# Graph layer with experts: output rows updated by an accumulating scatter in place of gather, add and scatter

## The chip, the cores and the metric

The kernel runs on one core of a Trainium2 chip. The metric is the time of one execution in microseconds of the device; the number for a kernel is the median of its runs. Five engines run side by side and are ordered only by semaphores: TensorE (PE, matmuls; PEld is its weight load), VectorE (DVE), ScalarE (ACT), GpSimd (POOL) and SyncE (SP), which issues most of the DMAs. The DMAs with indices are issued by GpSimd. All transfers share 16 DMA engines.

## What is computed

For 1250 nodes of 1024 features: a layer norm, then x + graph attention (20000 edges) + linear attention, then x + a mixture of 8 experts on the layer norm of that sum. Only the last part is touched by the change:

```python
x = x + gnn(xn, ...) + mix(xn, ...)
# experts, on the layer norm of x
scores = jnp.maximum((x @ gate_W + gate_b) / TEMP, EPS)
p = jax.nn.softmax(scores, axis=-1)
_, topk_idx = jax.lax.top_k(p, K)                      # K = 2 of E = 8
topk_mask = jax.nn.one_hot(topk_idx, E).sum(-2) > 0
w = jnp.maximum(p, W_THRES)
w = w / jnp.take_along_axis(w, topk_idx, axis=-1).sum(-1, keepdims=True)
comb = jnp.where(topk_mask, w, 0)
y = jnp.einsum('bsd,edf->bsef', x, expert_W) + expert_b
out = jnp.einsum('bsef,bse->bsf', y, comb) / K
x = x + out
```

All matmuls of weights are done with each float32 operand split in two parts, `hi` and `lo`, and three products.

## The kernel before

The kernel runs one stage after the other: the Gram matrix and linear attention, the attention table of the edges, the graph attention, then the layer norm and the gate, and last the experts. Up to the experts, `out` in HBM has been filled with x + graph attention + linear attention (line 529), and the normed rows lie in `xn2_d`.

**Routing (lines 1280 to 1361, VectorE).** Each of the 2500 pairs (token, chosen expert) gets a slot. Slots are ordered by expert, and every expert has whole blocks of 128 slots, at least one. `g_pos` is the slot of a pair. Slots that no pair fills are empty places; they stand at the end of an expert's last block. Two sets of small matmuls (line 1647, line 1666) turn positions into tables by slot: `tok_of` (which token), `slot_f` (the same as a float, -1 for an empty place), `row_of` (the output row; an empty place gets a row over N) and `w_slot` (its weight). `bounds` holds the first block of each expert. For these inputs the trace shows 23 blocks: experts 0 and 1 have one block each, expert 2 has eight (blocks 2 to 9), expert 3 one (block 10), experts 4 and 5 five each (11 to 15 and 16 to 20), experts 6 and 7 one each. This is read from where the casts of expert weights stand between the blocks.

**Experts.** Each engine has a loop over experts and, inside it, one over that expert's blocks.

- SP loads the weights of an expert as eight pieces of 512 KB into `e_raw[k]` (`load_expert`, line 531). There is one set of eight buffers: piece k of the next expert can be issued when VectorE has made `e_lo[k]` of the present one (`s_elo`). `load_bias` issues the bias.
- ScalarE casts them to `e_hi` (line 843, `expert_hi`), two buffers: expert e+1 is cast when all blocks of expert e-1 are multiplied. For each block it casts the transposed tokens to `lt_hi` (line 848) in two halves.
- VectorE, at the start of expert e and before its first block, makes `e_lo` of expert e+1 (line 1369, `expert_lo`, eight instructions). In block i it then does: the first half of `lt_lo` of block i+1 (line 1374), the two halves of `yb` = matmul result + bias (line 1421), the second half of `lt_lo`, and `y` = `yb` times `w_slot` plus `res` (line 1428). This order is fixed; a wait at `y` holds back everything after it.
- TensorE, in block i: 24 matmuls of the first half of the contraction, the 8 transposes of block i+1 (line 1655), 24 matmuls of the second half. It waits for `lt_lo` of its block (`s_llo`), and before it overwrites the result it waits for `yb` of the block before (`s_ye`).
- GpSimd, in block i: gathers the tokens of block i+2 into `gx` (line 654), gathers the output rows of block i into `res` (line 673), waits for `y` and scatters it to `out` (line 681), and skips rows over N. Blocks of one expert name different rows, so a gather of `res` needs to wait only for the scatter of the last block of the expert before (`s_sc` at `first_block[e]`, line 668). `y`, `res`, `gx` and `yb` each have one buffer.

Of the kernel before, what the change touches and what calls it, by code (L numbers as in the profile page):

```python
# [12 lines left out]
def gps_layer(nc, x, src, dst, gnn_W, gnn_a, w_ql, w_qr, w_key, w_value, gate_W, gate_b, expert_W, expert_b, out):  # L13
# [44 lines left out]
    with ctx:  # L58
        def at(name, word, shape, dt=f32):
            return nc.alloc_sbuf_tensor_at(name, shape, dt, offset=base + 4 * word)  # L60
# [133 lines left out]
        res = at("res", SMALL - D, [P, D])  # L194
# [71 lines left out]
        al_bc = at("al_bc", SH, [P, 2, P])  # L266
        al2 = small("al2", [P, NH, NT])
# [9 lines left out]
        row_now = small("row_now", [P, 1], i32)  # L277
# [115 lines left out]
        s_row, s_put, s_res, s_sum2, s_sc = sem("s_row"), sem("s_put"), sem("s_res"), sem("s_sum2"), sem("s_sc")  # L393
# [171 lines left out]
        def _(pool):  # L565
# [79 lines left out]
            for i in range(2):  # L645
                pool.wait_ge(s_xn2d[i], 16 * (NT // 2))
                pool.wait_ge(s_x2s[i], 16 * (NT // 2))
            pool.wait_ge(s_route, 1)
# [9 lines left out]
            first_block = [pool.value_load(bounds[0:1, e:e + 1], min_val=0, max_val=NBLK) for e in range(NE + 1)]  # L658
            pool.wait_ge(s_tr, 2)
            gather(1)  # L660
            pool.wait_ge(s_wslot, 1)
            pool.dma_start(res[:, :], out[0:P, :]).then_inc(s_sc, 16)
            for e in range(NE):

                with pool.Fori(first_block[e], first_block[e + 1]) as i:
                    pool.wait_ge(s_tr, i * 2 + 4)
                    gather(i + 2)
                    pool.wait_ge(s_sc, first_block[e] * 16 + 16)
                    pool.sem_inc(s_passed, 1)
                    nc.gpsimd.tensor_copy(row_now[:, :], row_of[:, bass.ds(i, 1)]).then_inc(s_row, 1)  # L670
                    pool.wait_ge(s_row, i + 1)
                    pool.sem_inc(s_passed, 1)
                    nc.gpsimd.indirect_dma_start(out=res[:, :], out_offset=None, in_=out,
                                                 in_offset=bass.IndirectOffsetOnAxis(ap=row_now[:, :], axis=0),
                                                 bounds_check=N - 1, oob_is_err=False).then_inc(s_res, 16)
                    pool.wait_ge(s_sum2, i + 2)
                    pool.sem_inc(s_passed, 1)
                    nc.gpsimd.tensor_copy(row_put[:, :], row_of[:, bass.ds(i, 1)]).then_inc(s_put, 1)
                    pool.wait_ge(s_put, i + 1)
                    pool.sem_inc(s_passed, 1)  # L680
                    nc.gpsimd.indirect_dma_start(out=out, out_offset=bass.IndirectOffsetOnAxis(ap=row_put[:, :], axis=0),
                                                 in_=y[:, :], in_offset=None,
                                                 bounds_check=N - 1, oob_is_err=False).then_inc(s_sc, 16)
            pool.wait_ge(s_gx, first_block[NE] * 16 + 32)
# [4 lines left out]
        def _(act):  # L689
# [167 lines left out]
            nc.scalar.activation(g_p[:, :, :], g_p[:, :, :], ACT.Exp).then_inc(s_gexp, 1)  # L857
            act.wait_ge(s_route, 1)
# [16 lines left out]
        def _(dve):  # L875
# [457 lines left out]
            link(V.tensor_tensor(g_place[:, :], g_cum[:, :], g_nb[:, :], ALU.subtract))  # L1333
            link(V.scalar_tensor_tensor(g_place[:, :], g_place[:, :], float(P), ps[:, 7, 0:NE], ALU.mult, ALU.add))
            link(V.scalar_tensor_tensor(g_place[:, :], g_place[:, :], -1.0, g_ends[:, 0:NE], ALU.add, ALU.subtract))
            link(V.tensor_tensor(g_pos[:, :, :], g_run[:, :, :].rearrange("p e t -> p t e"), over_tiles(g_place[:, :]), ALU.add))
# [68 lines left out]
            for g in range(2):  # L1405
                block_lo(0, g)
# [304 lines left out]
```

## Time and profile before

| | us |
|---|---|
| runs of the kernel before | 1359.47, 1359.84, 1362.1 (median 1359.84) |
| the profiled execution, its own time | 1355.7 |
| its span (first to last instruction) | 1353.4 |
| TensorE busy, share of the span | 1208.8 (89%) |
| VectorE | 757.0 (56%) |
| GpSimd | 441.8 (33%) |
| ScalarE | 306.0 (23%) |
| mean granted TensorE clock, share of full speed | 0.947 |

The experts' matmuls begin at 1021 us and end at 1342 us of the span. Times of start are counted from the start of the span. In the rows below a line gives the engine, the line of the kernel, the operation, what it writes and reads, and how many instructions were merged (`x8`). In brackets stands how long the engine was idle before and what ended the idle time. PE durations are those of one matmul from in to out and overlap; starts of matmuls in a row are what counts.

### The profile page before, as it was taken

The numbers are of one execution on the slowest core, as the hardware profiler recorded it, in microseconds if no ns is written. First come the engines' busy times: TensorE is split into PE (matmuls) and PEld (weight loads), VectorE is DVE, ScalarE is ACT, GpSimd is POOL, SyncE is SP. The second block draws the span as 40 slices with busy tenths as digits, with TensorE's granted clock in tenths as the row PEclk, the third lists the DMA queues.
The fourth block names the chain that finished last, engine by engine and source line by source line (L and its number), as shares of the span: only waits on it lengthen the run. The fifth ranks groups of instructions, "written<-read, shape, count | busy, mean of one in ns | idle before, by whom it ended". The sixth has DMA issues, their size and how long they took to land.

```text
span 1353.4 us, 16130 instructions
## 1 busy us (share of the span) xinstructions
PE 1208.8 (89%) x5789; PEld 1015.2 (75%) x5789; DVE 757.0 (56%) x1496; ACT 306.0 (23%) x410; POOL 441.8 (33%) x432
## 2 busy tenths in 40 slices
PE   5979799998999999999979999799937699889894
PEld 4878577776878899988967878688726588768683
DVE  7777531346333777767643247777567633553434
ACT  2321111113111111111012323233335211503030
POOL 4800587878784000000000035444202233233222
PEclk9989899998999999999989999799958799989997
DMA  5010241652412222211134441333358844663641
GB/s 190 17 47 1 87 128 37 219 159 73 125 15 80 82 82 83 96 51 57 51 103 141 136 125 70 121 106 119 125 207 314 331 139 134 231 233 128 236 138 60
DMA packets 89703, 165.02 MB, mean 122 GB/s; under 512 B 15468, under 2 KB 45926, under 8 KB 89508
## 3 DMA queue, kind: packets, MB, share of 16 engines
q1 hardware_dynamic: 74148, 129.76, 28.0%
q0 software_dynamic: 15488, 34.39, 8.6%
q8 instruction: 39, 0.64, 0.2%
q14 instruction: 28, 0.23, 0.0%
HBM read 125.53 MB, written 42.04 MB: 124 GB/s over the span
## 4 chain that ended last, share of the span: by engine, by line
PE 55%; DVE 13%; DMA 13%; issue 11%; POOL 5%; ACT 1%; POOLq 1%; DVEq 0%; SPq 0%; ACTq 0%
PE ps L1444 17%; PE ps L1445 17%; PE ps L1446 17%; DMA res<-out,row_now 9%; DMA out<-y,row_put 2%; DVE y L1428 2%; PE ps L1567 2%; POOL x_in L633 1%; DVE e_lo L1369 1%; DVE run L959 1%; PE ps L1629 1%; DVE w_lo L887 1%; DVE xt_lo L895 1%; DVE place_sum L1007 1%; DVE place L1005 1%
## 5 line engine op out<-in xcount | busy, mean ns | idle before, releaser
L595 POOL DMA_INDIRECT tab_d<-val_i,addr_i x160 | 213.5, 1334 | 144.7 <-issue 144.7
L1444 PE MATMUL ps<-e_hi,lt_hi 128*128 128x512 f32 x368 | 151.9, 413 | 41.6 <-DVE lt_lo L1374 41.6
L1446 PE MATMUL ps<-e_hi,lt_lo 128*128 128x512 f32 x368 | 147.9, 402 | 0.0
L1445 PE MATMUL ps<-e_lo,lt_hi 128*128 128x512 f32 x368 | 147.8, 402 | 0.0
L1444 PE MATMUL ps<-xt_hi,q_hi 128*128 128x416 f32 (+1 forms) x384 | 142.4, 371 | 0.0
L1445 PE MATMUL ps<-xt_lo,q_hi 128*128 128x416 f32 (+1 forms) x384 | 135.3, 352 | 0.0
L613 POOL TENSOR_TENSOR att_part<-att 128x640 f32<-128x640 f32 x10 | 16.9, 1687 | 362.1 <-PE ps L1446 358.1
L1446 PE MATMUL ps<-xt_hi,q_lo 128*128 128x416 f32 (+1 forms) x384 | 134.9, 351 | 0.0
L1444 PEld LDWEIGHTS ps<-e_hi,lt_hi 128*128 128x128 f32 x368 | 72.4, 197 | 58.8 <-DVE lt_lo L1374 44.5
L1134 DVE TENSOR_TENSOR cnt<-ps,cnt 128x256 f32 x208 | 87.7, 422 | 42.3 <-PE ps L1567 27.7
L1114 DVE TENSOR_SCALAR hot_s<-iota_g,s_tab 128x256 f16<-128x256 f16 x208 | 63.4, 305 | 39.9 <-PE ps L1567 39.1
L1428 DVE SCALAR_TENSOR_TENSOR y<-yb,w_slot,res 128x1024 f32<-128x1024 f32 x23 | 29.5, 1285 | 99.0 <-DMA res<-out,row_now 99.0
L1446 PEld LDWEIGHTS ps<-e_hi,lt_lo 128*128 128x128 f32 x368 | 71.8, 195 | 16.0
L1445 PEld LDWEIGHTS ps<-e_lo,lt_hi 128*128 128x128 f32 x368 | 72.6, 197 | 14.5
L848 ACT CAST lt_hi<-ps 128x512 fp32r<-128x512 f32 x48 | 28.1, 585 | 240.8 <-PE ps L1655 129.4
L1444 PE MATMUL ps<-h_hi,att_hi 128*128 128x512 f32 (+1 forms) x200 | 80.4, 402 | 0.0
L1445 PE MATMUL ps<-h_lo,att_hi 128*128 128x512 f32 (+1 forms) x200 | 79.5, 397 | 0.0
L1446 PE MATMUL ps<-h_hi,att_lo 128*128 128x512 f32 (+1 forms) x200 | 79.2, 396 | 0.0
L1369 DVE TENSOR_TENSOR e_lo<-e_raw,e_hi 128x1024 fp32r<-128x1024 f32 x64 | 73.4, 1221 | 4.1 <-ACT e_hi L843 4.1
L1444 PEld LDWEIGHTS ps<-xt_hi,q_hi 128*128 128x128 f32 x384 | 72.4, 188 | 1.8
L1445 PEld LDWEIGHTS ps<-xt_lo,q_hi 128*128 128x128 f32 x384 | 72.6, 189 | 0.5
L1446 PEld LDWEIGHTS ps<-xt_hi,q_lo 128*128 128x128 f32 x384 | 72.1, 188 | 0.5
(281 smaller groups left out, 2629.3 us busy)
## 6 DMA issues: line engine op xcount, KB each, us to landing
e_raw<-in_L_ffn_expert_W SPq DMA_DIRECT2D x64, 512.0 KB, 7.5
acc<-in_x SPq DMA_DIRECT2D x18, 512.0 KB, 7.8
w_raw<-in_L_mix_w_key SPq DMA_DIRECT2D x16, 512.0 KB
h_d<-hs SPq DMA_DIRECT2D x18, 256.0 KB
q_in<-q_d SPq DMA_DIRECT2D x9, 512.0 KB, 4.9
h_in<-h_d SPq DMA_DIRECT2D x9, 512.0 KB, 5.8
mix_d<-ms SPq DMA_DIRECT2D x18, 256.0 KB
mix_in<-mix_d SPq DMA_DIRECT2D x9, 512.0 KB, 3.3
```

The lines of the kernel that those rows point to most:

```text
L595: nc.gpsimd.indirect_dma_start(out=tab_d, out_offset=bass.IndirectOffsetOnAxis(ap=addr_i[0:EP, j:j + 1], axis=0), in_=val_i[0:EP, j:j + 1] ...
L613: nc.gpsimd.tensor_tensor(att_part[:, :, :], z[:, 0:half_t, :], z[:, half_t:NT, :], ALU.add).then_inc(s_part, 1)
L633: nc.gpsimd.tensor_tensor(v, v, mix_in[0:ROWS[i], i % 2, :], ALU.add).then_inc(s_xm, 1)
L848: nc.scalar.copy(lt_hi[:, MB * g:MB * g + MB, :], ps[:, 4 + g, :].rearrange("p (b c) -> p b c", c=P)).then_inc(s_lhi, 1)
L1114: V.tensor_scalar(hot_s[:, s, :], iota_g[:, :], s_tab[:, q:q + 1], None, ALU.is_equal)
L1134: V.tensor_tensor(o, ps[:, 7, j * GS:(j + 1) * GS], o, ALU.add).then_inc(s_cadd, 1)
L1369: V.tensor_tensor(e_lo[e % 2][:, k, :], e_raw[k][:, :], e_hi[e % 2][:, k, :].bitcast(f32), ALU.subtract).then_inc(s_elo, 1)
L1428: V.scalar_tensor_tensor(y[:, :], yb[:, :], w_slot[:, bass.ds(i, 1)], res[:, :], ALU.mult, ALU.add).then_inc(s_sum2, 1)
L1444: nc.tensor.matmul(o, lh, rh, start=(k == 0), stop=False)
L1445: nc.tensor.matmul(o, lh, rl, start=False, stop=False)
L1446: return nc.tensor.matmul(o, ll, rh, start=False, stop=(k == last_k))
L1567: last = nc.tensor.matmul(ps[:, 7, j * GS:(j + 1) * GS], hot_d[:, s, :], hot_s[:, s, :], start=True, stop=True)
```

## The change

Each block's product `yb * w_slot` is now scattered with an add onto `out`; the gather of output rows into `res` and its wait are gone, and so is the loop over experts on GpSimd. Since each scatter reads and writes `out`, every scatter waits for the one before. Every place of a block now takes part in the scatter, with weight 0 where it is empty, and an add needs 128 different rows in one scatter. So the empty places get rows of tokens that are not in that block: VectorE, GpSimd, TensorE and ScalarE together work out, for each expert, a ranking of rows outside its last block (rank by prefix sums over two groups of 128 tokens), and place the first of them in the empty places (`pad_*`). `row_of` is now the sum of the table of these and `slot_f`.

```diff
@@ GpSimd, between the waits for xn2_d and out and the wait for the routing
+            pool.wait_ge(s_gpos, 1)
+            step(G.tensor_scalar(last_p[:, :], g_cum[:, :], -1.0, float(P), ALU.add, ALU.mult))
+            G.tensor_scalar(last_b[:, :], g_cum[:, :], -1.0, None, ALU.add)
+            step(G.tensor_tensor(pad_in[:, :, :], g_pos[:, 0:2, :], over_two(last_p[:, :]), ALU.subtract))
+            step(G.tensor_scalar(pad_in[:, :, :], pad_in[:, :, :], 0.0, -1.0, ALU.is_ge, ALU.mult))
+            step(G.tensor_tensor(pad_in[:, :, :], pad_in[:, :, :], g_mask[:, 0:2, :], ALU.mult))
+            step(G.tensor_scalar(pad_in[:, :, :], pad_in[:, :, :], 1.0, None, ALU.add))
+            G.tensor_tensor(pad_n[:, :], pad_in[:, 0, :], pad_in[:, 1, :], ALU.add).then_inc(s_non, 1)
             pool.wait_ge(s_route, 1)
...
             gather(0)
+            pool.wait_ge(s_pre, 1)
+            step(G.tensor_tensor(pad_at[:, 0, :], pad_pre[:, :], pad_0[:, :], ALU.add))
+            step(G.tensor_tensor(pad_at[:, 0, :], pad_at[:, 0, :], last_p[:, :], ALU.subtract))
+            step(G.tensor_tensor(pad_at[:, 1, :], pad_at[:, 0, :], pad_in[:, 0, :], ALU.add))
+            step(G.tensor_scalar(pad_ok[:, :, :], pad_at[:, :, :], float(P), None, ALU.is_lt))
+            step(G.tensor_tensor(pad_ok[:, :, :], pad_ok[:, :, :], pad_in[:, :, :], ALU.mult))
+            G.tensor_tensor(pad_t[:, :, :], pad_ok[:, :, :], tokv[:, 0:2].unsqueeze(2).to_broadcast([P, 2, NE]),
+                            ALU.mult).then_inc(s_padt, 1)
             pool.wait_ge(s_tr, 2)
             gather(1)
-            pool.wait_ge(s_wslot, 1)
-            pool.dma_start(res[:, :], out[0:P, :]).then_inc(s_sc, 16)
-            for e in range(NE):
-                with pool.Fori(first_block[e], first_block[e + 1]) as i:
...
+            pool.wait_ge(s_rows, 1)
+            pool.dma_start(out_seen[:, :], out[0:P, 0:NE]).then_inc(s_sc, 16)
+            with pool.Fori(0, blocks) as i:
+                pool.wait_ge(s_tr, i * 2 + 4)
+                gather(i + 2)
+                pool.wait_ge(s_sc, i * 16 + 16)
+                nc.gpsimd.tensor_copy(row_put[:, :], row_of[:, bass.ds(i, 1)]).then_inc(s_put, 1)
+                pool.wait_ge(s_sum2, i + 2)
+                pool.wait_ge(s_put, i + 1)
+                nc.gpsimd.indirect_dma_start(out=out, out_offset=bass.IndirectOffsetOnAxis(ap=row_put[:, :], axis=0),
+                                             in_=y[:, :], in_offset=None, compute_op=ALU.add).then_inc(s_sc, 16)
@@ ScalarE, before the experts
+            act.wait_ge(s_nonp, 1)
+            nc.scalar.copy(pad_pre[:, :], ps[:, 6, 0:NE]).then_inc(s_pre, 1)
@@ VectorE, routing: one instruction more on 8 columns (pad_0); then behind tok_w and ahead of expert_lo(0)
+            dve.wait_ge(s_padt, 1)
+            V.tensor_tensor(last_c[:, :, :], io16[:, 0:NSLOT].unsqueeze(1).to_broadcast([P, NE, NSLOT]),
+                            last_b[:, :].unsqueeze(2).to_broadcast([P, NE, NSLOT]), ALU.is_equal)
+            link(V.tensor_tensor(pad_r[:, :, :, :].rearrange("p t e s -> p (t e) s"), ..., ALU.is_equal))   # 128 x 2048, f16
+            for c in range(2):
+                last = V.tensor_tensor(pad_c[:, c, :, :], last_c[:, :, :], pad_t[:, c, :].unsqueeze(2).to_broadcast([P, NE, NSLOT]), ALU.mult)
+            last.then_inc(s_pad, 1)
             expert_lo(0)
-            link(V.tensor_scalar(slot_e[:, :], slot_f[:, :], 0.0, 8192.0, ALU.is_lt, ALU.mult))
-            V.tensor_tensor(row_of[:, :], slot_f[:, :], slot_e[:, :], ALU.add)
             for g in range(2):
                 block_lo(0, g)
+            dve.wait_ge(s_padp, 1)
+            V.tensor_tensor(row_of[:, :], ps[:, 6, 64:64 + NSLOT], slot_f[:, :], ALU.add).then_inc(s_rows, 1)
@@ VectorE, in the loop over blocks
                     dve.wait_ge(s_sc, i * 16 + 16)
-                    dve.wait_ge(s_res, i * 16 + 16)
                     dve.wait_ge(s_ye, i * 2 + 4)
-                    V.scalar_tensor_tensor(y[:, :], yb[:, :], w_slot[:, bass.ds(i, 1)], res[:, :],
-                                           ALU.mult, ALU.add).then_inc(s_sum2, 1)
+                    V.tensor_scalar(y[:, :], yb[:, :], w_slot[:, bass.ds(i, 1)], None, ALU.mult).then_inc(s_sum2, 1)
@@ TensorE
+            pe.wait_ge(s_non, 1)
+            nc.tensor.matmul(ps[:, 6, 0:NE], tri2[:, :], pad_n[:, :], start=True, stop=True).then_inc(s_nonp, 1)
...
+            pe.wait_ge(s_pad, 1)
+            for c in range(2):
+                for e in range(NE):
+                    last = nc.tensor.matmul(ps[:, 6, 64:64 + NSLOT], pad_r[:, c, e, :], pad_c[:, c, e, :], ...)
+            last.then_inc(s_padp, 1)
```

## Rows read from the trace of the kernel before

**Rows 1.** stretches: us, engines' busy us, granted clock, DMA share, GB/s

```profile
1054.00:1074.00 20.00, 14.05 (x57) 11.26 (x57) 13.38 (x15) 6.93 (x8) 5.89 (x7) 0.84 0.79 299
1082.00:1159.00 77.00, 77.00 (x369) 64.36 (x368) 26.60 (x33) 7.62 (x13) 24.40 (x42) 1.00 0.41 132
```

**Rows 2.** waits after 1021 us: total us, times, longest

```profile
DVE y L1428 <- DMA res<-out,row_now: 99.0, 22, 6.9
PE ps L1444 <- DVE lt_lo L1374: 41.6, 8, 7.1
```

**Rows 3.** timeline, TensorE: start us, us, operation [idle before <- releaser]

```profile
1021.48 0.80 PE L1444 MATMUL ps<-e_hi,lt_hi 128*128 128x512 f32 x1 [6.89 <-DVE lt_lo L1374]
...
1036.74 0.47 PE L1444 MATMUL ps<-e_hi,lt_hi 128*128 128x512 f32 x1 [1.73 <-DVE lt_lo L1374]
...
1175.05 0.77 PE L1444 MATMUL ps<-e_hi,lt_hi 128*128 128x512 f32 x1 [4.05 <-DVE lt_lo L1374]
1175.62 0.63 PE L1445 MATMUL ps<-e_lo,lt_hi 128*128 128x512 f32 x1
1188.23 0.39 PE L1446 MATMUL ps<-e_hi,lt_lo 128*128 128x512 f32 x1
1194.24 0.77 PE L1444 MATMUL ps<-e_hi,lt_hi 128*128 128x512 f32 x1 [5.62 <-DVE lt_lo L1374]
```

**Rows 4.** timeline of VectorE, change of expert at block 10, last yb

```profile
1159.96 0.69 DVE L1374 TENSOR_TENSOR lt_lo<-ps,lt_hi 128x512 fp32r<-128x512 f32 x1
1163.38 1.28 DVE L1428 SCALAR_TENSOR_TENSOR y<-yb,w_slot,res 128x1024 f32<-128x1024 f32 x1 [2.73 <-DMA res<-out,row_now]
1164.59 9.17 DVE L1369 TENSOR_TENSOR e_lo<-e_raw,e_hi 128x1024 fp32r<-128x1024 f32 x8
1173.67 0.69 DVE L1374 TENSOR_TENSOR lt_lo<-ps,lt_hi 128x512 fp32r<-128x512 f32 x1
1174.27 1.28 DVE L1421 TENSOR_TENSOR yb<-ps,bias 128x512 f32<-128x512 f32 x2
...
1342.01 0.69 DVE L1421 TENSOR_TENSOR yb<-ps,bias 128x512 f32<-128x512 f32 x1 [2.03 <-PE ps L1446]
```

**Rows 5.** timeline, ScalarE: token casts, a weight cast

```profile
1100.38 0.59 ACT L848 CAST lt_hi<-ps 128x512 fp32r<-128x512 f32 x1 [5.38 <-PE ps L1446]
1112.18 0.59 ACT L848 CAST lt_hi<-ps 128x512 fp32r<-128x512 f32 x1 [5.41 <-PE ps L1446]
1183.48 1.06 ACT L843 CAST e_hi<-e_raw 128x1024 fp32r<-128x1024 f32 x1 [0.15 <-DMA e_raw<-in_L_ffn_expert_W]
```

**Rows 6.** timeline, GpSimd: first scatter, next row_now, last scatter

```profile
1046.32 1.06 POOL L681 DMA_INDIRECT out<-y,row_put  x1 [0.95 <-POOL row_put L678]
1052.92 0.39 POOL L670 COPY row_now<-row_of 128x1 int32 x1 [3.34 <-DMA out<-y,row_put]
1345.86 1.02 POOL L681 DMA_INDIRECT out<-y,row_put  x1 [0.92 <-POOL row_put L678]
```

**Rows 7.** the tile res: time of its DMAs from issue to landing

```profile
DMA to landing us min/median/max: 3.2/4.9/8.4
```

**Rows 8.** line 1275, duration ns min, median, max

```profile
L1275 DVE TENSOR_SCALAR xn<-x_in,mv,nt x10: 812/1034/1041, 834.4 to 979.5; 128x1024 f32<-128x1024 f32 x9, 98x1024 f32<-98x1024 f32 x1
```

**Rows 9.** groups of GpSimd instructions: total us, mean ns

```profile
L617 POOL TENSOR_TENSOR att_part<-att_part 128x128 f32<-128x128 f32 x10 | 6.9, 689 | 0.8
L651 POOL COPY tok_now<-tok_of 128x1 int32 x23 | 5.9, 257 | 9.7 <-PE ps L1655 9.6
```

**Rows 10.** timeline of VectorE: routing and the start of the experts

```profile
999.57 1.49 DVE L1352 TENSOR_TENSOR tok_r<-io,p_lo 128x1280 f16<-128x1280 f16 x1
1009.31 2.11 DVE L1398 TENSOR_TENSOR tok_w<-tok_s,w_part 128x580 bf16<-128x580 bf16 x3
1011.34 9.17 DVE L1369 TENSOR_TENSOR e_lo<-e_raw,e_hi 128x1024 fp32r<-128x1024 f32 x8
1020.42 0.18 DVE L1403 TENSOR_SCALAR slot_e<-slot_f 128x29 f32<-128x29 f32 x1
```

More of the change, by code:

```diff
@@ L192, in gps_layer @@
         assert EX + 6 * D <= RAW
-        res = at("res", SMALL - D, [P, D])
+        pad_r = at("pad_r", SMALL - D, [P, 2, NE, P], f16)
+        last_c = at("last_c", EX + 3 * D, [P, NE, NSLOT], f16)
+        pad_c = at("pad_c", EX + 3 * D + HALF, [P, 2, NE, NSLOT], f16)
         G = RAW
@@ L266, in gps_layer @@
         al_bc = at("al_bc", SH, [P, 2, P])
+        last_p = at("last_p", SH, [P, NE])
+        last_b = at("last_b", SH + 8, [P, NE])
+        pad_0 = at("pad_0", SH + 16, [P, NE])
+        pad_pre = at("pad_pre", SH + 24, [P, NE])
+        pad_n = at("pad_n", SH + 32, [P, NE])
+        pad_in = at("pad_in", SH + 40, [P, 2, NE])
+        pad_at = at("pad_at", SH + 56, [P, 2, NE])
+        pad_ok = at("pad_ok", SH + 72, [P, 2, NE])
+        pad_t = at("pad_t", SH + 88, [P, 2, NE])
+        out_seen = at("out_seen", SH + 104, [P, NE])
         al2 = small("al2", [P, NH, NT])
@@ L276, in gps_layer @@
         tok_now = small("tok_now", [P, 1], i32)
-        row_now = small("row_now", [P, 1], i32)
         row_put = small("row_put", [P, 1], i32)
@@ L392, in gps_layer @@
         s_passed = sem("s_passed")
-        s_row, s_put, s_res, s_sum2, s_sc = sem("s_row"), sem("s_put"), sem("s_res"), sem("s_sum2"), sem("s_sc")
+        s_put, s_sum2, s_sc = sem("s_put"), sem("s_sum2"), sem("s_sc")
+        s_gpos, s_non, s_nonp, s_pre, s_padt, s_pad, s_padp, s_rows, s_step = (sem(n) for n in (
+            "s_gpos", "s_non", "s_nonp", "s_pre", "s_padt", "s_pad", "s_padp", "s_rows", "s_step"))
         s_chain = sem("s_chain")
@@ L647, in _, with step, over_two @@
                 pool.wait_ge(s_x2s[i], 16 * (NT // 2))
+            steps = [0]
+            def step(i):
+                steps[0] += 1
+                i.then_inc(s_step, 1)
+                pool.wait_ge(s_step, steps[0])
+            def over_two(v):
+                return v.unsqueeze(1).to_broadcast([P, 2, NE])
+            G = nc.gpsimd
+            pool.wait_ge(s_gpos, 1)
[6 more added lines that the diff above has]
+            G.tensor_tensor(pad_n[:, :], pad_in[:, 0, :], pad_in[:, 1, :], ALU.add).then_inc(s_non, 1)
             pool.wait_ge(s_route, 1)
@@ L663, in _ @@
-            for e in range(NE):
-                with pool.Fori(first_block[e], first_block[e + 1]) as i:
[L666 to L683, printed above, removed]
@@ L685, in _ @@
+            pool.wait_ge(s_gx, blocks * 16 + 32)
             pool.sem_inc(s_passed, 1)
@@ L1668, in _ @@
             last.then_inc(s_wsum, 1)
+            pe.wait_ge(s_pad, 1)
+            for c in range(2):
+                for e in range(NE):
+                    last = nc.tensor.matmul(ps[:, 6, 64:64 + NSLOT], pad_r[:, c, e, :], pad_c[:, c, e, :],
+                                            start=(c + e == 0), stop=(c == 1 and e == NE - 1))
+            last.then_inc(s_padp, 1)
             for e in range(NE):
```

12 lines of the change are left out of this document (9 added, 3 removed).

## The prediction

> **What bounds the kernel now.** I read the page first: TensorE is busy for 89% of the span, but the chain that ended last names `res<-out,row_now` for 9% of the span, a gather that only exists in the experts. So I went to the experts' stage and read three views there. The view of stretches [rows 1] shows two kinds of time. From 1082 to 1159 us, inside expert 2, TensorE is busy 77.0 of 77 us at a granted clock of 1.00: the reader is to see that nothing else matters there. From 1054 to 1074 us, around experts of one block, it is busy 14.05 of 20 us at 0.84. The waits [rows 2] name the reason in two steps. VectorE waited 99.0 us at line 1428 for `res`, in 22 of 23 blocks, and TensorE waited 41.6 us in 8 places for `lt_lo`, which VectorE makes. The 99 us are no loss by themselves; inside an expert VectorE has time to wait. At a change of expert it has not. The timeline of VectorE shows one [rows 4]: the second half of `lt_lo` is ready at 1160.65 (1159.96 + 0.69), `y` starts only at 1163.38 when `res` has landed, then come the eight `e_lo` of the next expert, 9.1 us, then `lt_lo` and `yb`, and TensorE restarts at 1175.05 after 4.05 us of idle time [rows 3]. For the first block of an expert the wait is longer, since the gather of `res` waits for the last scatter and then takes its own time beside the weight loads: up to 8.4 us [rows 7].
>
> **The ideal and the excess.** A block inside an expert takes 11.8 us (casts of the same half at 1100.38 and 1112.18) [rows 5], 23 of them 271.4 us. From the first matmul of the experts at 1021.48 [rows 3] to the last one's end, a tenth of a microsecond before the last `yb` at 1342.01 [rows 4], there are 320.4 us. The excess is 49.0 us. Of it 34.7 us are TensorE's idle time behind the first restart (41.6 - 6.9) [rows 2, 3]. The other 14.3 us are matmuls at the lower clock: after a restart from 4 to 7 us of idle time a matmul lasts 0.63 us where it is else 0.39 [rows 3], for the first 6 to 13 of them, and a block lasts 13.6 us (1175.05 to 1188.6) or more. Seven restarts are of that kind, 2.0 us each. The eighth, at 1036.74 after 1.73 us, is not: its first matmul takes 0.47 us and the clock stays at 2.4 GHz.
>
> **What the change removes.** `y` waits no more for `res`. What is late next at a change of expert? By the same row pattern [rows 4], from the start of `y` to TensorE's restart there are 1175.05 - 1163.38 = 11.67 us. `y` can now start at 1160.65, and is shorter: its nearest row is line 1275, a tensor_scalar of the same shape, 1.03 us in place of 1.28 [rows 8]. So the restart would come at 1160.65 + 11.67 - 0.25 = 1172.1, and TensorE ends the block before at 1171.0 (restart less its idle time) [rows 3]. Idle: 1.1 us where it was 4.05. At a change behind an expert of one block the same reckoning gives 0.7 to 0.9 us; I take 1.0 for each of the six changes. Gaps of 1.0 us are shorter than the 1.73 us that left the clock alone, so I charge no lower clock. Two other things must keep up. The cast `e_hi` of ScalarE depends on weight pieces that can be issued when `e_lo` is made. In the trace the `e_lo` block at block 10 ends at E = 1173.76, which frees the last buffer, and the cast of the piece loaded there starts at 1183.48 and ends at E + 10.8 [rows 4, 5]. In the new order VectorE does `lt_lo`, two `yb`, `lt_lo` and `y` behind E, some 3.35 us (1.28 + 0.69 + 1.03 and the first `lt_lo`, overlapped by a tenth each), then seven `e_lo` of 1.14 us, and wants that cast at E + 11.3. So it is just in time, with 0.5 us to spare; I charge nothing and keep it for the second rival. And the pieces keep their pace, since one 512 KB gather leaves the queues for each add that enters them. New excess: 1.7 + 6 x 1.0 idle and one cold start of 2.0, 9.7 us. **Gain in the experts: 49.0 - 9.7 = 39.3 us.**
>
> **What it adds ahead of the experts.** All of this stands on VectorE between `tok_w` and `e_lo` [rows 10], which is the path: TensorE waited 6.9 us for the first `lt_lo`. `tok_r` takes 1.49 us for 1280 columns of f16 [rows 10], so 1.1 ns a column; `pad_r` has 2048 and takes 2.3 us, `last_c` and two `pad_c` have 232 each and take about 0.35 us each in a row. That is 3.35 us. Another 0.2 us is `pad_0`, and 0.3 us leave with `slot_e` (0.18 us) and the old `row_of`, of which 0.2 come back behind `lt_lo`. Next the wait for `s_padt`. GpSimd has seven small operations before the routing is known and six after the first token gather. No row shows such shapes there. From below a copy of one column takes 0.26 us on average, from above a tensor_tensor of 128 columns 0.69 us [rows 9]; I take 0.5 us, nearer the upper since these are also two-operand instructions. The first seven, 3.5 us from about 996.5, are hidden beside 8 us of routing on VectorE. The six take 3.3 us from 1007.6, that is to 1010.9, and VectorE is at the wait at 1011.6. With the upper price and VectorE in the way it would be 1013; I take 0.5 us of wait, bounds 0 to 4. The two matmul groups and the copy on ScalarE lie where those engines idle: cost 0, at most 0.5. Sum: 3.3 + 0.2 + 0.5 - 0.1, **3.9 us lost**, bounds 3 to 8. The preload of `res`, 512 KB, becomes 4 KB; nothing waits for it.
>
> **The scatter with an add** is the unknown: no row shows one. Queued behind its landing are the next `y` (one buffer) on VectorE and, on GpSimd, the next scatter; behind `y` stand `expert_lo` and so TensorE. Per block the chain is `y` 1.03, about 0.9 us from its end to the issue (the idle time before a scatter) [rows 6], and the landing L. It hides as long as 1.03 + 0.9 + L is under 11.8: L up to 9.9 us. Bounds of L: from below the landing of a plain gather of the same 512 KB, 4.9 us as median and 3.2 at the least [rows 7]. From above a read and a write one after the other beside weight loads: 8.4 us [rows 7] plus the scatter's 6.4 (1046.32 to the idle time's end at 1052.7) [rows 6], 14.8 us. Added to that, the rows of empty places now move too, 444 of 2944. Inside an expert the queues are 41% busy [rows 1], and I take L = 7; beside weight loads I take 9.5, since reads and writes of different rows overlap. Both hide. 
>
> **Sum.** 39.3 - 3.9 - 1.8 = 33.6 us of gain. On the profiled execution's own 1355.7 us that is 1322.1. The median of the runs is 1359.84, 4.1 above it, so the forecast is 1326.2 us.
>
> **Rivals.**
> *The landing of the add paces every block.* Place: VectorE's `y`, waiting for the scatter of the block before. It decides from L = 9.9 us on, costs 22 x (L - 9.9), and eats the gain at L = 11.4. At the upper bound of 14.8 us it is 108 us less 34: 1434; at 13 us 1394. For it: nothing in the trace shows how an add reads and writes, and GpSimd builds its descriptors. Against: gathers and scatters take 4.9 and 6.4 us today, and half the queue time is free. I give it 0.15 and a middle of 1395.
> *Only the adds beside weight loads are late.* At the changes behind blocks 1, 2, 10 and 11 a landing of 12 to 13 us holds `y` back by 2 to 3 us, TensorE's gap grows to 3 or 4 us and the lower clock comes back with 2 us. Four times 5 us: 1346. The same time comes out if the weight pieces are the limit there (the margin above is 1 us). For it: gathers take 8.4 us there against 4.9 [rows 7], at 299 GB/s of traffic [rows 1]. Chance 0.21.
> *The change does little*: the gap at a change of expert is set by loads or by the front work growing to the upper bounds, and everything comes to within 0.2% of before. Chance 0.02.
>
> **How the numbers follow.** 0.62 for the forecast, whose own range is 1317 to 1335 (front 3 to 8, tail 0 to 7, gaps of 0.7 to 1.5 us). With the second rival this reaches 1352, and about 2 in 10 lie outside: range 1316 to 1356. What a measurement of this kernel can tell from no change is about 0.2%. Faster 0.82 (the forecast, nearly all of the second rival), same 0.02, slower 0.16.
>
> **What would show it.** Right: the wait of VectorE at `y` gone or under 10 us in all; six restarts of TensorE after about 1 us with 0.39 us matmuls from the start; the first expert matmul near 1025.4; blocks inside an expert still 11.8 us. Wrong: blocks of more than 11.8 us inside expert 2 with `y` waiting for the scatter (the first rival); gaps of 3 us and more behind blocks 1, 2, 10 and 11 only (the second); a wait of VectorE ahead of `last_c` of over 4 us (GpSimd's small operations).

## The result and the profile after

The changed kernel takes 1323.56 us (median of 4 runs, 1321.35 to 1324.85) against 1359.65 us (median of 4, 1359.27 to 1362.1): a ratio of 0.9736, 95% interval 0.972 to 0.9752. The forecast was 1326.2 us. The profiled execution has a span of 1321.6 us where it was 1353.4, 31.8 us less; the medians differ by 36.1, since the profiled execution of the kernel before, with 1355.7 us, was 4 us under its median and that of the changed kernel, with 1323.36, was at it. Split at four marks that both traces have:

| stretch | before | after | difference | forecast |
|---|---|---|---|---|
| start to the copy of the gate's scores (`sc`), not touched | 987.53 | 989.87 | +2.34 | 0 |
| to the first expert matmul | 33.95 | 37.19 | +3.24 | +3.9 |
| to the start of the last `yb` | 320.5 | 282.5 | -38.0 | -39.3 |
| to the end of the span | 11.39 | 12.04 | +0.65 | +1.8 |

The first row is no effect of the change: in two more executions of the same kernel that mark stood at 987.57 and 990.16.

First the experts' stage and parts of it, by the view of stretches of the changed kernel. Columns: the stretch, its length, the busy time (and instructions) of PE, PEld, DVE, ACT and POOL, then granted clock, DMA share and GB/s.

```profile
1027.06:1309.56 282.50, 275.55 (x1288) 227.04 (x1288) 139.70 (x172) 78.58 (x99) 82.37 (x92) 0.99 0.66 192
1054.00:1075.00 21.00, 19.38 (x93) 15.64 (x93) 14.60 (x17) 9.51 (x11) 10.54 (x6) 1.00 1.03 389
1082.00:1150.00 68.00, 68.00 (x325) 56.76 (x324) 18.91 (x28) 6.45 (x11) 17.81 (x24) 1.00 0.47 93
```

TensorE is idle for 282.50 - 275.55 = 6.95 us of the stage. The same stretch of before (1021.48 to 1342.01) has 320.53 us with 285.82 busy at a clock of 0.94, 34.7 idle. So 27.8 us of the gain are idle time and 10.3 us are busy time that the lower clock had stretched. Where the loss was worst, around the experts of one block, TensorE was busy 14.05 of 20 us at a clock of 0.84 [rows 1]. It is now busy 19.38 of 21 at 1.00, although the DMA engines are full there (1.03, 389 GB/s).

The waits after 1021 us (engine, line, for what: total us, times, longest) answer to [rows 2]:

```profile
DVE y L1470 <- DMA out<-y,row_put: 8.3, 3, 4.5
...
PE ps L1485 <- DVE lt_lo L1410: 11.8, 5, 9.1
PE ps L1698 <- DMA gx<-xn_d,tok_now: 3.3, 2, 2.2
```

VectorE's 99.0 us at `y` have become 8.3. Of TensorE's 11.8 us for `lt_lo`, 9.07 belong to the first matmul of the experts; the other 2.7 are four short gaps. New is the third row: transposes that wait for a late gather of tokens. The change of expert at block 10 in VectorE's timeline (start, us, operation), against [rows 4]:

```profile
1151.12 0.69 DVE L1410 TENSOR_TENSOR lt_lo<-ps,lt_hi 128x512 fp32r<-128x512 f32 x1
1151.73 0.75 DVE L1470 TENSOR_SCALAR y<-yb,w_slot 128x1024 f32<-128x1024 f32 x1
1152.39 9.17 DVE L1405 TENSOR_TENSOR e_lo<-e_raw,e_hi 128x1024 fp32r<-128x1024 f32 x8
1161.48 0.68 DVE L1410 TENSOR_TENSOR lt_lo<-ps,lt_hi 128x512 fp32r<-128x512 f32 x1
```

`y` starts as soon as `lt_lo` is made; 2.73 us of idle time stood there before. And TensorE's restart behind it, against the 4.05 us and the 0.63 us matmuls of [rows 3]:

```profile
1162.86 0.47 PE L1485 MATMUL ps<-e_hi,lt_hi 128*128 128x512 f32 x1 [0.69 <-DVE lt_lo L1410]
```

The scatters, by the lines for the tile `out` (duration ns min, median, max; DMA to landing):

```profile
L714 POOL DMA_INDIRECT out<-y,row_put x23: 1598/1605/7289, 1044.4 to 1312.6; - x23
...
DMA to landing us min/median/max: 4.8/6.5/15.0
```

The price nobody could read before is the median: an add of 512 KB lands after 6.5 us. The instruction on GpSimd lasts 1.6 us where the plain scatter took 1.02 to 1.07. Surprising is the maximum of 7.3 us. Two of 23 are long, and both look like this in GpSimd's timeline:

```profile
1056.51 6.14 POOL L714 DMA_INDIRECT out<-y,row_put  x1 [2.84 <-DVE y L1470]
1062.09 1.67 POOL L684 COPY tok_now<-tok_of 128x1 int32 x1
1064.56 1.32 POOL L687 DMA_INDIRECT gx<-xn_d,tok_now  x1 [0.81 <-POOL tok_now L684]
1070.68 0.18 POOL L709 COPY row_put<-row_of 128x1 int32 x1 [4.79 <-DMA out<-y,row_put]
```

The long instruction holds back the gather of tokens behind it (the transposes then waited 1.10 us at 1073.09), and its landing comes at 1070.7, 14.2 us after the issue, so that the next `y` waits 3.27 us.

### The profile page after: what moved, and what is told of

Its sections match the earlier page's. It is cut to its first block, busy times and chain, and to the rows that moved or that the text cites. A ratio compares the mean times of both kernels' runs of the same rounds, so it can differ in the third digit from the quotient of the medians.

```text
span 1321.6 us, 16015 instructions
## 1 busy us (share of the span) xinstructions
PE 1201.5 (91%) x5807; PEld 1010.4 (76%) x5807; DVE 747.4 (57%) x1500; ACT 306.1 (23%) x411; POOL 435.2 (33%) x399
## 4 chain that ended last, share of the span: by engine, by line
PE 76%; DVE 13%; issue 4%; DMA 3%; POOL 2%; ACT 2%; DVEq 1%; SPq 0%; POOLq 0%; ACTq 0%
PE ps L1485 23%; PE ps L1486 23%; PE ps L1487 23%; DVE e_lo L1405 2%; PE ps L1608 2%; PE ps L1670 2%; PE ps L1698 1%; DVE run L993 1%; DMA gx<-xn_d,tok_now 1%; DVE w_lo L921 1%; DVE xt_lo L929 1%; PE ps L1572 1%; DVE place L1039 1%; DVE place_sum L1041 1%; ACT w_hi L728 1%
## 5 line engine op out<-in xcount | busy, mean ns | idle before, releaser
L1485 PE MATMUL ps<-e_hi,lt_hi 128*128 128x512 f32 x368 | 147.0, 399 | 12.6 <-DVE lt_lo L1410 11.8
L1487 PE MATMUL ps<-e_hi,lt_lo 128*128 128x512 f32 x368 | 144.3, 392 | 0.0
L1486 PE MATMUL ps<-e_lo,lt_hi 128*128 128x512 f32 x368 | 144.1, 391 | 0.0
L1168 DVE TENSOR_TENSOR cnt<-ps,cnt 128x256 f32 x208 | 87.3, 420 | 42.4 <-PE ps L1608 27.8
L1485 PEld LDWEIGHTS ps<-e_hi,lt_hi 128*128 128x128 f32 x368 | 69.6, 189 | 28.6 <-DVE lt_lo L1410 15.1
L1486 PEld LDWEIGHTS ps<-e_lo,lt_hi 128*128 128x128 f32 x368 | 69.8, 190 | 13.7
L714 POOL DMA_INDIRECT out<-y,row_put x23 | 47.2, 2052 | 92.4 <-DVE y L1470 87.0
```

What stands on the lines that cost most here:

```text
L1168: V.tensor_tensor(o, ps[:, 7, j * GS:(j + 1) * GS], o, ALU.add).then_inc(s_cadd, 1)
L1485: nc.tensor.matmul(o, lh, rh, start=(k == 0), stop=False)
L1486: nc.tensor.matmul(o, lh, rl, start=False, stop=False)
L1487: return nc.tensor.matmul(o, ll, rh, start=False, stop=(k == last_k))
```

## The experiments

Times are medians; the ratio is to the kernel before on the same chip, with its 95% interval. For the chip of the four runs from two adds to the free gather no run of the changed kernel is on record, so a difference to it of 2 or 3 us is no more than a hint there.

**The changed kernel again**, to learn what differs between executions.

> The changed kernel itself, unchanged, as the yardstick of the three others on the same chip. Both theories expect about 1323 us, 36 us under the kernel before.

Measured: 1322.91 us, ratio 0.9749 (0.9725 to 0.9773). No scatter over 1.7 us and no wait at `y` at all. But VectorE's `e_lo` of expert 3 waited for ScalarE's casts and these for the weight pieces, and TensorE stood still:

```profile
1059.22 2.50 DVE L1405 TENSOR_TENSOR e_lo<-e_raw,e_hi 128x1024 fp32r<-128x1024 f32 x2 [0.70 <-ACT e_hi L875]
1063.22 1.22 DVE L1405 TENSOR_TENSOR e_lo<-e_raw,e_hi 128x1024 fp32r<-128x1024 f32 x1 [1.50 <-ACT e_hi L875]
```

Its restart at 1065.93 came after 3.18 us. That is the "just in time" of the prediction, missed at one change of expert.

**A third execution of it.**

> The changed kernel again, a third profiled execution of it, to see how often a scatter instruction of GpSimd lasts long (7.29 and 6.14 us in the first, none over 1.7 us in the second). Theory A (chance alignment with VectorE's e_lo block): long ones only at the three places where a scatter is issued about 1 us into an e_lo block, in none, one or several of them; time 1321 to 1325 us. Theory B (a fixed place in the program, or weight traffic): the same two places as in the first, or any place beside a weight load.

Measured: 1325.39 us (one run). One scatter of 3.87 us at 1057.07, none long elsewhere; the late weight pieces now at block 11 (`e_lo` waits of 0.61, 0.83 and 1.64 us for ScalarE's casts, TensorE restarts at 1178.57 after 3.83 us). So neither event has a fixed place.

**The front work alone**: everything `pad_*` is computed in the kernel before, into a table that nobody uses.

```diff
+ all pad_* steps on GpSimd, VectorE, ScalarE and TensorE, as in the change
+ V.tensor_tensor(row_new[:, :], ps[:, 6, 64:64 + NSLOT], slot_f[:, :], ALU.add)   # gather, add, scatter go by the old row_of
```

> The kernel before plus all the front work of the change (the pad_ tables, their matmuls, the sum in a tile that nobody uses, and the wait of GpSimd for it), with the old gather of output rows, the wait for it and the plain scatter kept. Theory (front work stands on the path): 3.2 us slower than the kernel before, 1363. Rival (slack behind w_slot swallows it): within 1 us of before. A gain would mean that something in the front work helps, such as the 4.1 us hole of VectorE at 1022 us closing.

Measured: 1363.01 us, 1.0029 (1.0014 to 1.0044), 3.6 us more, as the theory said. From the copy of `sc` to the first expert matmul 37.47 us against 33.95.

**The change without the front work**: add and scatter as changed, but `row_of` as before with the bounds check, so that empty places are skipped.

```diff
- all pad_* steps
+ V.tensor_tensor(row_of[:, :], slot_f[:, :], slot_e[:, :], ALU.add)                   # rows over N, as before
- in_=y[:, :], in_offset=None, compute_op=ALU.add)
+ in_=y[:, :], in_offset=None, compute_op=ALU.add, bounds_check=N - 1, oob_is_err=False)
```

> The changed kernel without its work on empty places: row_of is made as before (an empty place names a row over 1250), the scatter with an add has the bounds check of the old scatter, and all pad_ work on GpSimd, VectorE, TensorE and ScalarE is gone. Theory (the gain is y no longer waiting for res at the changes of expert; the front work costs about 3.2 us on VectorE's path to the first expert matmul): 1320 us, 3 us under the changed kernel, with the first expert matmul 3.1 us earlier after the routing; the last scatter moves few rows again and gives back 0.5 us or so. Rival (the front work is hidden, because what stood behind w_slot in the kernel before had 4 us of slack): the same time as the changed kernel within 1 us.

Measured: 1320.92 us, 0.9724 (0.9708 to 0.9739), the fastest here of the kernels that do the whole computation. Its interval overlaps that of the changed kernel in the same comparison. The first expert matmul comes 33.91 us behind the copy of `sc`, so the 3.3 us are back, and the tail is 10.4 us where the changed kernel's three executions have 12.0, 11.6 and 11.5. But the experts' stage takes 286.6 us, 2 to 4 us more than with the front work, with one very long scatter at block 0, as the next timeline shows (GpSimd):

```profile
1039.14 9.49 POOL L686 DMA_INDIRECT out<-y,row_put  x1 [5.27 <-issue]
1048.03 0.80 POOL L664 COPY tok_now<-tok_of 128x1 int32 x1
```

and VectorE beside it:

```profile
1037.94 9.16 DVE L1375 TENSOR_TENSOR e_lo<-e_raw,e_hi 128x1024 fp32r<-128x1024 f32 x8
1047.02 0.68 DVE L1380 TENSOR_TENSOR lt_lo<-ps,lt_hi 128x512 fp32r<-128x512 f32 x1
```

TensorE's transposes wait 4.63 us for `gx` behind it, and the matmuls that follow them take 0.63 us. The other five changes of expert have scatters of 2.68 us. All six begin 1.15 to 1.21 us into an `e_lo` block.

**The same kernel again.**

> The kernel that leaves the empty places out again, to see how often the long scatter instructions come (9.49 us once and 2.68 us five times in its first profile). Theory A: those over 1.7 us all begin inside an e_lo block of VectorE, their number may differ. Theory B: the same instructions are long again. Time 1319 to 1322 us.

Measured: 1323.15 us (one run). The same six again: 9.48 us at block 0 and five of 2.68 us.

**The preload of `res` cut from 512 KB to 4 KB** in the kernel before.

```diff
-            pool.dma_start(res[:, :], out[0:P, :]).then_inc(s_sc, 16)
+            pool.dma_start(res[:, 0:NE], out[0:P, 0:NE]).then_inc(s_sc, 16)
```

> The kernel before with one edit: the preload of res (512 KB, behind w_slot) is 8 columns wide, 4 KB. Theory A (the 4.1 us hole of VectorE between w_slot and e_lo, and so the 1.73 us gap of TensorE at 1036.74, come from that preload or what it holds up): hole gone, 1.5 to 2 us faster than before. Theory B (the hole is something else, such as fetching of instructions): no change within 0.5 us, hole of about 4 us still there.

Measured: 1360.32 us, 1.0008 (0.9994 to 1.0022): no change, as theory B said. VectorE's 4.1 us hole before the second `e_lo` block stays.

**Two adds per block**: behind the first a second one of the same size, into a buffer in HBM that is no longer read.

```diff
+                in_=y[:, :], in_offset=None, compute_op=ALU.add).then_inc(s_first, 16)
+                pool.wait_ge(s_first, i * 16 + 16)
+                nc.gpsimd.indirect_dma_start(out=mix_d, ..., in_=y[:, :], in_offset=None, compute_op=ALU.add).then_inc(s_sc, 16)
```

> The changed kernel with a second scatter with an add of the same rows onto a spare tensor (mix_d), issued when the first has landed; y and the next scatter wait for the second. It doubles the landing that the chain from y to y has to hide. Theory (the landing of 6.3 us hides because y, issue and landing together stay under 11.8 us): the chain becomes 0.75 + 1.0 + 6.3 + about 1 + 6.3 = 15.3 us a block, so 3.5 us too long for 22 blocks, less some slack at the start: 65 to 80 us slower than the changed kernel, about 1395, and VectorE waits at y for the scatter in nearly every block. Rival (an add costs TensorE nothing whatever its landing, VectorE's work has more slack than that): under 20 us slower.

Measured: 1431.21 us, 1.0518 (1.0479 to 1.0557), a miss: about 108 us over the changed kernel where 65 to 80 had been worked out. The quiet blocks came as worked out, the ones beside weight loads did not. GpSimd in a quiet block:

```profile
1102.97 1.59 POOL L715 DMA_INDIRECT out<-y,row_put  x1 [1.53 <-DVE y L1475]
1109.97 1.55 POOL L719 DMA_INDIRECT mix_d<-y,row_put  x1 [5.41 <-DMA out<-y,row_put]
...
1116.22 0.18 POOL L710 COPY row_put<-row_of 128x1 int32 x1 [2.63 <-DMA mix_d<-y,row_put]
1117.93 1.59 POOL L715 DMA_INDIRECT out<-y,row_put  x1 [1.53 <-DVE y L1475]
```

A block takes 14.95 us, 15.3 had been worked out, and there the landing paces. Beside weight loads two adds need 22 us (1043.6 to 1066.2 to 1087.9), and TensorE waits 71.8 us in 21 places for `gx`, whose gather is queued behind the second scatter. This is the first rival made real: it decides when what `y` has to wait for is twice as long.

**The add left out of the scatter**, so that `out` holds only the last product of a row.

```diff
-                                             in_=y[:, :], in_offset=None, compute_op=ALU.add).then_inc(s_sc, 16)
+                                             in_=y[:, :], in_offset=None).then_inc(s_sc, 16)
```

> The changed kernel with the scatter as a plain write, no add: out then holds the last product alone, the sum with what stood there is left out. Theory (the add's landing and its longer GpSimd instruction hide): within 2 us of the changed kernel, 1321 to 1324; landing of the scatter 4 to 5 us inside an expert in place of 6.3, instruction 1.0 us in place of 1.6. Rival (the add's second read is what fills the DMA engines around experts of one block, where TensorE still waits 1 to 3 us for weights or tokens): 3 to 6 us faster than the changed kernel and no gaps over 1 us.

Measured: 1317.01 us, 0.9692 (0.965 to 0.9735), about 6 us under the changed kernel by the medians. The theory had 2 us at most; the rival had 3 to 6 us. The runs go from 1314.1 to 1321.3 us and the interval overlaps that of the changed kernel (0.972 to 0.9752), so the size is uncertain. Scatter instructions last 0.99 to 1.03 us, none is long, the waits for `gx` are 0.2 us in all. In the profiled execution, with 1314.2 us one of the two short ones of the four, the stage takes 277.7 us (1025.76 to 1303.48) and the tail 8.8 us. The three of the changed kernel have 282.5 to 284.7 us and 11.5 to 12.0. So the add costs about 3 us at the tail and up to 5 to 7 us in the stage. Part of the latter is late weight pieces, which come in some executions only.

**Small weight loads**: experts 2 to 7 load 128 of 1024 columns of each piece and multiply with stale weights in the rest.

```diff
-                    sp.dma_start(e_raw[k][:, :], expert_W[e, k * P:(k + 1) * P, :]).then_inc(s_er[k], 16)
+                    c = slice(0, D if e <= 1 else P)
+                    sp.dma_start(e_raw[k][:, c], expert_W[e, k * P:(k + 1) * P, c]).then_inc(s_er[k], 16)
```

> The changed kernel with weight pieces of experts 2 to 7 that load 128 of their 1024 columns; the products of those experts are of stale weights. Number and order of all instructions stay. Theory (what is left around experts of one block, scatter instructions of 6 to 9 us, landings of 14 to 15 us, gaps of 1 to 3 us, is the traffic of the weights): 3 to 5 us faster than the changed kernel, 1319, every scatter instruction at 1.6 us and landed within 7 us, gaps of TensorE only the 0.5 to 1.0 us of VectorE's own order. Rival (the long scatter instructions come from VectorE's e_lo that runs at the same time, or from the descriptors of the add themselves): they stay, and the time within 1 us.

Measured: 1322.55 us, 0.9727 (0.9686 to 0.9768): a miss: 1319 had been expected. Most of the weight traffic is gone (114 GB/s over the stage instead of 192), but a scatter of 9.56 us came all the same, with VectorE in the same place:

```profile
1164.12 9.56 POOL L715 DMA_INDIRECT out<-y,row_put  x1 [4.01 <-DVE y L1471]
1173.12 0.78 POOL L685 COPY tok_now<-tok_of 128x1 int32 x1
```

The eight `e_lo` run from 1163.04 to 1172.2. So a long instruction doesn't need the weight traffic. No `e_lo` waits for a cast in this profile, and TensorE's restarts behind `lt_lo` come after 0.72 us or less. That fits the late pieces of the second and third execution, though one profile can't exclude chance.

**The kernel before with a free gather**: `res` is gathered from `xn2_d`, which no scatter writes, and waits for none; the output lacks the right rows of x.

```diff
-                    pool.wait_ge(s_sc, first_block[e] * 16 + 16)
+                    pool.wait_ge(s_sc, 16)
-                    nc.gpsimd.indirect_dma_start(out=res[:, :], out_offset=None, in_=out,
+                    nc.gpsimd.indirect_dma_start(out=res[:, :], out_offset=None, in_=xn2_d,
```

> The kernel before with the gather of res reading xn2_d in place of out, so that it need not wait for the last scatter at a change of expert; the sum that it makes is of wrong rows, all instructions are the same. Theory (the gain of the change is the wait for res at a change of expert, made of two parts: the wait for the last scatter, 3 to 4 us on GpSimd, and the landing of the gather itself, 7 to 8 us beside weight loads): about half to two thirds of the gain, 20 to 28 us faster than the kernel before, 1332 to 1340, with y still waiting 2 to 4 us at changes. Rival (the gather was only late because of the wait for the scatter): all of it, 1323 to 1326. Other rival (the gain came from removed traffic, not from the wait): no change.

Measured: 1343.79 us, 0.9889 (0.985 to 0.9927), 16 us of gain (10 to 20 by the interval) and not 20 to 28. `y` still waits 62.5 us in 21 blocks for `res`, and TensorE 24.0 us in 7 places for `lt_lo`. So less than half of the gain is the order of gather behind scatter; the rest comes only when the gather itself is gone.

**`e_lo` waits for the scatter's issue**, in the changed kernel and in the one that skips empty places. Both are for these inputs alone, since the numbers of blocks are written in as constants.

```diff
+                nc.gpsimd.memset(issued[:, :], 0.0).then_inc(s_issued, 1)          # GpSimd, behind each scatter
...
+                if 1 <= e < NE - 1:                                                # VectorE, before expert_lo(e + 1)
+                    dve.wait_ge(s_issued, (0, 1, 2, 10, 11, 16, 21)[e])
```

> The changed kernel, but VectorE's e_lo block of the next expert waits until GpSimd has issued the scatter of the block before. Theory A (the scatter instruction is held up by VectorE's e_lo instructions, two fp32 inputs from SBUF): no scatter instruction over 1.7 us and no landing over 12 us. Theory B (something else holds it up): a scatter of 6 us or more can still come. In both, e_lo starts some 2.3 to 2.7 us later at six changes of expert, lt_lo follows it one to one, and TensorE waits 3 to 3.5 us there instead of 0.7: 6 x 2.5 = 15 us more, less up to 3.3 us of late gathers: 1332 to 1338 us; about 1346 us if idle of 3.4 us already lowers the granted clock at each of them (2.0 us each).

> The same wait in the kernel that leaves the empty places out. Theory A: scatter instructions of 1.6 us at the changes too, none of 2.68 or 9.49 us. Theory B: they come as before. Time by the same terms: 1321 + 15 less up to 4.6 us of the late gather and six times 1.1 us of the 2.68 us scatters as far as they paced anything: 1329 to 1336 us.

Measured: 1338.44 us, 0.9851 (0.9823 to 0.9879), and 1334.97 us, 0.9818 (0.9788 to 0.9848). The scatters of the first, then of the second:

```profile
L715 POOL DMA_INDIRECT out<-y,row_put x23: 1599/1605/1666, 1043.7 to 1327.6; - x23
```

```profile
L687 POOL DMA_INDIRECT out<-y,row_put x23: 1602/1606/1652, 1042.1 to 1328.3; - x23
...
DMA to landing us min/median/max: 4.5/6.3/8.2
```

None is long. Of the second kernel without the wait all six at a change of expert were, in both executions. The longest landing falls from 17.1 to 8.2 us. The next weight loads follow `e_lo` and so were moved too, so this alone doesn't part the instruction from the queues. The trace of the changed kernel does, from the issue to the next `row_put`: 14.2 and 15.2 us less the 4.5 and 5.7 us by which those two instructions are too long are 9.6 and 9.5, and the short ones beside weight loads have 8.1 to 10.5. The wait itself costs more than it saves, by the mechanism of [rows 4]: what holds `e_lo` back holds `lt_lo` and TensorE back (first kernel, VectorE and then TensorE):

```profile
1060.50 2.36 DVE L1407 TENSOR_TENSOR e_lo<-e_raw,e_hi 128x1024 fp32r<-128x1024 f32 x2 [2.75 <-POOL issued L717]
```

```profile
1055.99 0.77 PE L1489 MATMUL ps<-e_hi,lt_hi 128*128 128x512 f32 x1 [3.45 <-DVE lt_lo L1412]
1056.55 0.63 PE L1490 MATMUL ps<-e_lo,lt_hi 128*128 128x512 f32 x1
```

In the first kernel's stage of 298.43 us TensorE is idle for 14.6 us (6.95 in the changed kernel) and busy for 283.80 (275.55), so half of the 16 us is the lower clock again; it came behind four gaps of about 3.5 us and not behind all six changes, which is why the time lies between the two figures expected. The first kernel moves no byte more than the changed one, and gives back 15 of its 36 us by the order on VectorE alone.

## Why the prediction was right, step by step

**The excess of the experts.** Right: forecast 9.7 us, 282.5 - 271.4 = 11.1 measured, against 49.0 before. The blocks inside expert 2 still start every 11.8 us (`y` at 1104.57 and 1116.35). The idle part was forecast as 7.7 us and is 6.95, but made of other pieces. The gap at block 1 is gone together with VectorE's hole; the six changes of expert cost 0.29 to 0.71 us where 1.0 was charged; and 3.3 us are the late gathers, a step that the prediction did not have. The lower clock was forecast as one cold start, 2.0 us; busy time beyond the ideal is 275.55 - 271.4 = 4.15 us. Of it the first block has 2.2: its first matmul starts at 1027.06 and that of the next block at 1041.09, 14.03 us later. The other 1.9 us lie in the ten blocks at and just behind the changes of expert, 0.1 to 0.3 us each with matmuls of 0.39 us; their cause was not looked for. "Gaps of 1 us leave the clock alone" held in this execution: each first matmul behind them takes 0.47 us and the following ones 0.39.

**`y` without `res`.** Forecast 1.03 us from line 1275; it takes 0.736 to 0.754 us. The nearest row was too dear, on the safe side: 0.3 us at each change of expert, which is what makes the gaps shorter than 1.0.

**The weight pieces "just in time, 0.5 us to spare".** This is the weakest step, and it held only in part. The shorter `y` takes up most of the margin: the `e_lo` block at 1152.39 ends at 1161.56 and the next one starts at 1164.54, 2.98 us behind it where 3.35 was reckoned, so the last cast is wanted at about E + 10.9 and not at E + 11.3. (The second rival gives this margin as 1 us, the working as 0.5.) In the first execution the pieces were nearly in time: two blocks of eight `e_lo` took 9.6 and 9.4 us in place of 9.17. In the second they cost 3.18 us at one change and in the third 3.83 us at another, both with matmuls at the lower clock behind them. The second rival named four places at 5 us each; one place in two of three executions is what came. The stage took 282.5, 284.7 and 284.7 us. That the first execution escaped is luck, worth about 2 us.

**The front work.** Forecast 3.9 us, 3.24 in the trace of the change, 3.52 and 3.6 us in the run of it alone, and 3.3 us come back when it is left out. Its parts in VectorE's timeline:

```profile
1013.98 0.40 DVE L1438 TENSOR_TENSOR last_c<-io,last_b 128x232 f16<-128x232 f16 x1
1014.29 2.29 DVE L1440 TENSOR_TENSOR pad_r<-io,pad_at 128x2048 f16<-128x2048 f16 x1
1016.61 0.71 DVE L1443 TENSOR_TENSOR pad_c<-last_c,pad_t 128x232 f16<-128x232 f16 x2
```

The price by column from `tok_r` [rows 10] gave 2.3 us for `pad_r` and it took 2.29. No idle time precedes `last_c`: the 0.5 us of wait for GpSimd's small operations did not come. GpSimd's operations on 8 or 16 columns last 0.20 to 0.36 us, below both rows of [rows 9] in most cases, so the value should have been taken at the lower end.

**The landing of the add.** Forecast 7 us inside an expert and 9.5 beside weight loads, with 9.9 as the point where it is felt. Measured 6.3 to 6.8 us in quiet blocks inside expert 2, to the next `row_put` (issue 1094.51, `row_put` at 1100.79). Beside weight loads there were 8.1 to 10.5 us, and 14.2 and 15.2, which are the long instructions: 15.2 less the 5.7 us by which it is too long is 9.5. So the sizes were right, and what the prediction missed is a reason for late landings that is not in the queues. The Trainium skill, "Collectives: The Full Stack", section on why ReduceScatter is half of AllGather, says an add needs two source reads. That agrees in direction: leaving the add out took some 3 us off the tail. The quiet landing with it is only 1.6 us over the plain gather's median of 4.9 [rows 7]. A gather is another transfer, though, and no view here gives the landing of the plain scatter, so the rate itself is not measured.

**The tail.** Forecast +1.8, measured +0.65. From the last `yb` to the issue of the last scatter 3.04 us against 3.85, 0.8 saved (0.6 forecast); from there to the end 9.0 against 7.5, 1.5 more (2.4 forecast). In the other two executions the tail was 11.6 and 11.5 us, 0.1 to 0.2 over before.

**The sum.** The three stretches that the change touches gained 34.1 us where 33.6 was forecast. Part of this closeness is cancelling: the experts gave 1.3 us less, the front work and the tail cost 0.7 and 1.1 us less. The profiled execution took 1323.36 us, 1322.1 had been worked out; the 4.1 us added for the median were not needed, since the changed kernel's median is 1323.56.

**What stays open.** Before the change VectorE stood for 4.1 us between `w_slot` and the `e_lo` block of expert 1. It does so in the kernels with the small preload, the free gather, the front work alone and the skipped empty places (with and without the wait); it does not in the changed kernel, with the wait, with two adds, without the add, or with small loads. Neither the preload nor the front work alone decides it, and the cause was not found. It cost at most 1.7 us at block 1.

## What to carry to other kernels

A read, change and write of rows in HBM has two costs, the transfers and the order between them; when the engine that waits for the read also makes the operands of the next stage in program order, an accumulating scatter takes the read off that path, and here that was worth 38 of 320 us although the transfers themselves were mostly hidden. Price it by asking how long the one buffer is held (here 1.7 us from the start of `y` to the issue and 6.3 us of landing, against a block of 11.8 us). Try the bounds check together with the add before building a table of harmless rows: leaving the empty places out saved 3.3 us of front work, of which 2 us were left in the medians (1320.92 against 1322.91 us on one chip, intervals that overlap).

## What the runs showed of the hardware

**A scatter with an add can be held up beside a run of VectorE instructions.** The instruction takes 1.55 to 1.67 us when VectorE is not in a run of tensor_tensor instructions on two SBUF tiles, and in such a run anything up to 9.56 us, for the longest until 1.5 us after the run of eight ends. With the run moved behind it, 12 of 12 were short; without, 6 of 6 were long twice (empty places skipped), 2, 0 and 1 of 6 in three executions of the changed kernel and 1 of 6 with small loads. What follows `e_lo`, the next weight loads and casts, moved with it, so the run itself is the likely cause and not the only thing that was changed; the amount of traffic is ruled out by the small loads.

The traces show one thing more, the moment of the start. The second `e_lo` of a run starts 1.13 us after the first. In the kernel that skips empty places all 12 scatters began just behind that, 1.15 to 1.21 us into the run, and all were long. In the changed kernel, with small loads and with two adds (the first add of a block), 30 began just ahead of it or with it, 1.05 to 1.13 us into the run, and 4 were long. These kernels differ in the bounds check too, so that the moment decides is not shown, and why 4 of the 30 are long is open.

A copy of one column on GpSimd takes 0.18 to 0.23 us alone and up to 1.72 us beside `e_lo`. No plain scatter was long (0.99 to 1.08 us, 30 of them in an `e_lo` run), but all of these began at the start of an `e_lo` instruction or up to 0.1 us ahead of it, none just behind it, so that a plain scatter is safe there is not shown. The Trainium skill, "SBUF — State Buffer", section "Who interferes with whom", says that a VectorE instruction with two SBUF inputs contends with a GpSimd instruction that reads SBUF, and infers that writing descriptors is not hit by it. The first half agrees with the copies. For the scatter with an add the runs show that the instruction is held up (9.49 us in place of 1.6); what inside it waits, they don't show.

**The clock after short idle times.** Every restart after up to 1.7 us of idle time kept 2.4 GHz. After 3.45 us (above) the next matmuls took 0.63 us, after 3.18 us the first one took 0.77. The first matmul alone can mislead: behind the 3.83 us in the third execution of the changed kernel it took 0.47 us, as after a short gap, and the slow ones came two matmuls later:

```profile
1178.57 0.47 PE L1485 MATMUL ps<-e_hi,lt_hi 128*128 128x512 f32 x1 [3.83 <-DVE lt_lo L1410]
1178.87 0.40 PE L1486 MATMUL ps<-e_lo,lt_hi 128*128 128x512 f32 x1
1179.11 0.57 PE L1487 MATMUL ps<-e_hi,lt_lo 128*128 128x512 f32 x1
1179.47 0.63 PE L1485 MATMUL ps<-e_hi,lt_hi 128*128 128x512 f32 x1
```

The granted clock of the 5 us from 1178.57 is 0.66. In the kernel that waits and skips it is 0.66 behind a gap of 3.01 us (1069.41) and 1.00 behind one of 3.09 us (1054.35); with small loads it is 0.66 behind 2.52 us (1181.75), with two adds 1.00 behind 3.75 us (1299.17). So in these kernels the length of one gap of 2.5 to 3.75 us doesn't tell the outcome. Look at the granted clock of the stretch behind a restart, not at its first matmul.
